# Another order of the feed-forward turns' steps, and two scratch tensors laid out in pieces of 1 KB

## What is computed

```python
x = x + attn(layernorm(x))        # _ska_block, itself with a residual
x = x + ffn(layernorm(x))         # 256 -> 1024 -> gelu -> 256, binarized weights

# attn, per chunk and head (Q, K, V: 128 x 64)
G = K.T @ K + 1e-4 * I
W = solve(G, K.T @ V)
U = I[:, :8]
for _ in range(2): U, _ = qr(W @ U)
Wr = U @ (U.T @ W)
S = 0.9 * S + Wr                   # state over the 8 chunks of a sequence
out = 0.125 * (Q @ S)
```

## Time and profile before

| | us |
|---|---|
| median of 3 runs | 900.69 |
| lowest and highest | 897.38, 904.1 |
| the profiled execution, its own time | 900.93 |
| its span | 899.1 |
| PE busy | 783.1 (87%) |
| DVE busy | 631.7 (70%) |
| ACT busy | 490.1 (55%) |
| POOL busy | 227.4 (25%) |

### The profile page before, as it was taken

One profiled execution on the slowest core, in us unless ns is written; L12 is line 12 of the kernel. 1 busy time (PEld: TensorE's weight loads), 2 busy tenths in 40 slices (PEclk: granted clock), 3 DMA queues, 4 the chain that ended last, 5 costly groups with the idle time before them and its releaser, 6 DMA issues.

```text
span 899.1 us, 34359 instructions
## 1 busy us (share of the span) xinstructions
PE 783.1 (87%) x14730; PEld 530.6 (59%) x14730; DVE 631.7 (70%) x1336; ACT 490.1 (55%) x1068; POOL 227.4 (25%) x297
## 2 busy tenths in 40 slices
PE   4999999999999998988687687888798888899996
PEld 2555555565555555656455565666576666677775
DVE  3666399089998999980798988889953304666664
ACT  1864444555455454554444465556566665466665
POOL 4666100201001100000201012652012203555554
PEclk9999999999999999999879888999999999899999
DMA  8555211653455636655734645344456432222210
GB/s 313 155 159 167 77 62 42 205 177 122 139 162 160 185 72 168 185 162 168 162 79 119 188 116 159 103 135 116 107 154 138 104 93 69 62 82 74 77 43 30
DMA packets 174662, 114.43 MB, mean 127 GB/s; under 512 B 134128, under 2 KB 152944, under 8 KB 173488
## 3 DMA queue, kind: packets, MB, share of 16 engines
q1 hardware_dynamic: 168784, 91.00, 36.8%
q0 software_dynamic: 5728, 21.24, 7.5%
HBM read 61.22 MB, written 50.99 MB: 125 GB/s over the span
## 4 chain that ended last, share of the span: by engine, by line
PE 66%; DVE 13%; issue 9%; DMA 5%; ACT 4%; SPq 1%; POOL 1%; POOLq 0%; DVEq 0%; ACTq 0%
PE psum L1286 25%; PE psum L1332 6%; PE psum L1531 6%; PE psum L1541 5%; DVE outer L1142 4%; PE psum L1473 3%; PE psum L1511 3%; DVE work L1148 3%; PE psum L1504 2%; PE psum L1388 2%; PE psum L1375 2%; PE psum L1362 2%; PE psum L1423 2%; DVE state L1204 2%; PE psum L1497 1%
## 5 line engine op out<-in xcount | busy, mean ns | idle before, releaser
L1286 PE MATMUL psum<-wkv,xhat 128*128 128x512 f32 x512 | 240.3, 613 | 4.3 <-ACT xhat L834 4.3
L1142 DVE SCALAR_TENSOR_TENSOR outer<-work,rd 128x992 f32<-128x992 f32 (+30 forms) x248 | 189.6, 764 | 8.9 <-DVE rd L1136 0.3
L1148 DVE TENSOR_TENSOR work<-work,outer 128x992 f32<-128x992 f32 (+30 forms) x248 | 176.3, 711 | 8.6
L1286 PEld LDWEIGHTS psum<-wkv,xhat 128*128 128x128 f32 x512 | 93.2, 192 | 105.3 <-issue 99.5
L871 ACT COPY kv<-psum 128x512 f32<-128x512 f32 x128 | 75.1, 587 | 120.8 <-PE psum L1286 120.5
L1002 ACT ACTIVATE late<-psum,b1c,alpha 128x128 f32<-128x128 f32 x256 | 96.7, 461 | 49.6 <-PE psum L1531 49.6
L759 POOL TENSOR_TENSOR hsplit<-late,hsplit 128x512 f16<-128x512 f32 x64 | 77.4, 1211 | 142.4 <-ACT hsplit L1007 142.3
L1531 PEld LDWEIGHTS psum<-y3t,s1t 128*128 128x128 f16 x1024 | 61.3, 102 | 17.7 <-issue 16.7
L1531 PE MATMUL psum<-y3t,s1t 128*128 128x128 f16 x1024 | 66.9, 227 | 4.4 <-DVE y3t L1232 4.0
L1541 PE MATMUL psum<-s2t,hsplit 128*128 128x256 f16 x512 | 63.7, 279 | 4.0 <-POOL hsplit L759 2.7
L1332 PE MATMUL psum<-kv 128*64 128x128 f32 x1024 | 64.4, 280 | 0.0
(11 more groups left out here) (130 smaller groups left out, 1279.5 us busy)
## 6 DMA issues: line engine op xcount, KB each, us to landing
gc_d<-gc SPq DMA_DIRECT2D x32, 384.0 KB, 2.5
schur_mem<-gc_d SPq DMA_DIRECT2D x32, 384.0 KB, 4.2
f_d<-late SPq DMA_DIRECT2D x16, 512.0 KB, 3.6
late<-f_d SPq DMA_DIRECT2D x32, 256.0 KB, 2.7
sv_d<-sv SPq DMA_DIRECT2D x16, 384.0 KB, 3.1
lead_d<-work POOLq DMA_DIRECT2D x4, 1024.0 KB, 5.0
schur_mem<-lead_d SPq DMA_DIRECT2D x32, 128.0 KB, 4.3
r_d<-pt SPq DMA_DIRECT2D x16, 256.0 KB, 2.2
```

What stands on the lines that cost most here:

```text
L1142: V.scalar_tensor_tensor(out=tile, in0=a[:, t, t + 1:HALF].unsqueeze(2).broadcast_to([P, m, HALF]), scalar=rd[:, t:t + 1], in1=a[:, t, t + ...
L1148: V.tensor_tensor(rest, rest, tile, ALU.subtract).then_inc(swept, 1)
L1286: ins = mm(dst[:], xnt[:, c, t], wkv[:, n, t, BANK * half:BANK * (half + 1)], start=t == 0, stop=t == KT - 1)
```

## The change

There are two parts.

**Order.** The turn's steps are appended in another sequence: AU (one chunk's operator) moves from behind GE0 to directly behind OUT; NB is taken one chunk further ahead (`r + 3`); X3 stands behind NB; and Y3 moves from behind AU to directly behind HID, ahead of GE0. Two DVE weights of the planner are larger. The mask step MB of a sequence waits in the plan until the NB steps of the sequence before last are placed. Since the planner interleaves all streams, the list changes from its 303rd PE step on.

**Layout.** `pt`, `r_d` and `rr` now hold the head index innermost, and `sv`, `sv_d` hold the 32-wide parts of a chunk first and the 64-wide parts behind, so that the reads of `rr` and `vv` are contiguous pieces of 1 KB per partition. For that SP and SX write PSUM with a step of 8 elements, SX and W read `pt` and `rr` with that step, `lt` is written by ACT with a step of 32 elements, and the copy of SV becomes two.

```diff
-DVE_WEIGHT = dict(AU=.75, AT=1.4, X3=.45, Y3=.5, OUT=.95)
+DVE_WEIGHT = dict(AU=.75, AT=1.4, X3=.8, Y3=.5, OUT=1.45)
-                if t <= now["pe"]:
+                if t <= now["pe"] and (b < 2 or ("NB", CPB * (b - 1) - 1) in where):
-        for step, n in (("LF", r + 4), ("LO1", r - 1), ("AT", r + 1), ("LR", r + 3), ("OUT", r - 2), ("X3", r + 1), ("NB", r + 2),
-                        ("HID", r), ("GE0", r), ("AU", r + 2), ("LO0", r), ("Y3", r + 1), ("GE1", r)):
+        for step, n in (("LF", r + 4), ("LO1", r - 1), ("AT", r + 1), ("LR", r + 3), ("OUT", r - 2), ("AU", r + 2), ("NB", r + 3),
+                        ("X3", r + 1), ("HID", r), ("Y3", r + 1), ("GE0", r), ("LO0", r), ("GE1", r)):
-    r_d = scratch("r_d", [NCH, P, PAIRS, HALF])
-    sv_d = scratch("sv_d", [NCH, P, PAIRS // 2, 3 * HALF])
+    r_d = scratch("r_d", [NCH, P, HALF, PAIRS])
+    sv_d = scratch("sv_d", [NCH, P, PAIRS // 2 * 3 * HALF])
...
-                    sp.dma_start(vv[:, i], sv_d[c + i][:, :, HALF:]).then_inc(solve_loaded, 16)
+                    sp.dma_start(vv[:, i], sv_d[c + i][:, P:].rearrange("p (s n) -> p s n", n=HD)).then_inc(solve_loaded, 16)
-                    sp.dma_start(rr[:, i, :, 0:HALF], r_d[c + i]).then_inc(sides_loaded, 16)
+                    sp.dma_start(rr[:, i, 0:HALF], r_d[c + i]).then_inc(sides_loaded, 16)
...
-                    nc.scalar.mul(lt[rows(2 * a)].rearrange("p c h n -> p (c h n)"), src[rows(2 * a)], -1.0)
+                    nc.scalar.mul(lt[rows(2 * a)].rearrange("p c h n -> p c n h"),
+                                  src[rows(2 * a)].rearrange("p (c n h) -> p c n h", c=2, h=PAIRS), -1.0)
-                nc.scalar.copy(sv[:].rearrange("p c s n -> p c (s n)"), pieces(place("SV", e), BANK)[:, :, 0:12 * HALF]
-                               ).then_inc(drain("SV", e), 1)
+                src = pieces(place("SV", e), BANK)[:, :, 0:12 * HALF].rearrange("p c (s n) -> p c s n", n=3 * HALF)
+                nc.scalar.copy(sv[:, :, 0:P].rearrange("p c (s n) -> p c s n", n=HALF), src[:, :, :, 0:HALF])
+                nc.scalar.copy(sv[:, :, P:].rearrange("p c (s n) -> p c s n", n=HD), src[:, :, :, HALF:]).then_inc(drain("SV", e), 1)
...
-                            ins = mm(dst[sl, at:at + HALF], lp[sl, c, h, HALF:], lp[sl, c, h, 0:HALF], start=True, stop=True)
+                            ins = mm(dst[sl, c, :, h], lp[sl, c, h, HALF:], lp[sl, c, h, 0:HALF], start=True, stop=True)
...
-                                r, u = rr[side(a), c % 2, 2 * q + n], cu[side(a), n, c % 2, q]
+                                r, u = rr[side(a), c % 2, :, 2 * q + n], cu[side(a), n, c % 2, q]
```

More of the change, by code:

```diff
@@ L374, in build @@
         w2n = schur_mem[:, FT * DM:FT * DM + KT * FF].rearrange("p (t h) -> p t h", h=FF)
-        pt = sb("pt", [P, 2, 2, PAIRS, HALF])
-        xg = pt[:].rearrange("p e c h n -> p (e c h n)").rearrange("p (a k d) -> p a k d", a=2, k=2)
+        pt = sb("pt", [P, 2, 2, HALF, PAIRS])
+        xg = pt[:].rearrange("p e c n h -> p (e c n h)").rearrange("p (a k d) -> p a k d", a=2, k=2)
         lt = sb("lt", [P, 2, PAIRS, HALF])
-        sv = sb("sv", [P, 2, PAIRS // 2, 3 * HALF])
+        sv = sb("sv", [P, 2, PAIRS // 2 * 3 * HALF])
         lps = sb("lps", [P, 2, PAIRS // 2, HD])
         vv = sb("vv", [P, 2, PAIRS // 2, HD])
-        rr = sb("rr", [P, 2, PAIRS, HD])
+        rr = sb("rr", [P, 2, HD, PAIRS])
         cu = sb("cu", [P, 2, 2, PAIRS // 2, HD])
@@ L562, in load_solve @@
                 if e == 0:
-                    sp.wait_ge(eyes_placed, 4)
+                    sp.wait_ge(eyes_placed, 6)
                 if e % HALF_BATCH == 0:
@@ L618, in _ @@
                     sp.wait_ge(*is_drained("SX", c))
-                    sp.dma_start(r_d[2 * c:2 * c + 2].rearrange("c p h n -> p c h n"), pt[:, c % 2]
+                    sp.dma_start(r_d[2 * c:2 * c + 2].rearrange("c p n h -> p c n h"), pt[:, c % 2]
                                  ).then_inc(r_stored[c % 2], 16)
@@ L622, in _ @@
                     sp.wait_ge(*is_drained("SV", c))
-                    sp.dma_start(sv_d[2 * c:2 * c + 2].rearrange("c p s n -> p c s n"), sv[:]).then_inc(sv_stored, 16)
+                    sp.dma_start(sv_d[2 * c:2 * c + 2].rearrange("c p n -> p c n"), sv[:]).then_inc(sv_stored, 16)
                 elif step == "LS":
@@ L709, in load_sweep @@
                     for s in range(PAIRS // 2):
-                        src = sv_d[CPB * b:CPB * (b + 1), :, s, 0:HALF].rearrange("c (q i) n -> (c q) i n", q=QUADS)
+                        src = sv_d[CPB * b:CPB * (b + 1), :, HALF * s:HALF * (s + 1)].rearrange("c (q i) n -> (c q) i n", q=QUADS)
                         pool.dma_start(buf[rows(s), :, 0:HALF], src).then_inc(sweep_loaded[j], 16)
@@ L800, in place_eyes @@
                     eye = ident[sl, sl].unsqueeze(1).broadcast_to([HALF, 2 * PAIRS, HALF])
-                    nc.scalar.copy(rr[sl, :, :, HALF:].rearrange("p a h n -> p (a h) n"), eye).then_inc(eyes_placed, 1)
+                    for i in range(2):
+                        nc.scalar.copy(rr[sl, i, HALF:], ident[sl, sl].unsqueeze(2).broadcast_to([HALF, HALF, PAIRS])
+                                       ).then_inc(eyes_placed, 1)
                     nc.scalar.copy(lt[sl].rearrange("p a h n -> p (a h) n"), eye).then_inc(eyes_placed, 1)
@@ L894, in leading_inverse @@
                 wait(act, r_stored[e % 2], 16 * (e // 2))
-                nc.scalar.copy(pt[:, e % 2].rearrange("p c h n -> p (c h n)"), place("SP", e)).then_inc(drain("SP", e), 1)
+                nc.scalar.copy(pt[:, e % 2].rearrange("p c n h -> p (c n h)"), place("SP", e)).then_inc(drain("SP", e), 1)
             def crosses(e):
@@ L902, in crosses @@
                 for a in range(2):
-                    nc.scalar.mul(lt[rows(2 * a)].rearrange("p c h n -> p (c h n)"), src[rows(2 * a)], -1.0)
+                    nc.scalar.mul(lt[rows(2 * a)].rearrange("p c h n -> p c n h"),
+                                  src[rows(2 * a)].rearrange("p (c n h) -> p c n h", c=2, h=PAIRS), -1.0)
                 for a in range(2):
-                    ins = nc.scalar.mul(pt[rows(2 * a + 1), e % 2].rearrange("p c h n -> p (c h n)"), src[rows(2 * a + 1)], -1.0)
+                    ins = nc.scalar.mul(pt[rows(2 * a + 1), e % 2].rearrange("p c n h -> p (c n h)"), src[rows(2 * a + 1)], -1.0)
                 ins.then_inc(drain("SX", e), 1)
@@ L1354, in leading_inverse @@
             def leading_inverse(e):
-                dst = begin("SP", e)
+                dst = begin("SP", e).rearrange("p (c n h) -> p c n h", c=2, h=PAIRS)
                 pe.wait_ge(schur_loaded[e % 2], 64 * (e // 2 + 1))
@@ L1369, in crosses @@
                     for h in range(PAIRS):
-                        at = HALF * (PAIRS * c + h)
                         for turned in range(2):
@@ L1373, in crosses @@
                                 sl = rows(2 * a)
-                                p, b = pt[sl, e % 2, c, h], gct[sl, e % 2, c, h, 0:HALF]
-                                ins = mm(dst[rows(2 * a + turned), at:at + HALF], b if turned else p, p if turned else b,
+                                p, b = pt[sl, e % 2, c, :, h], gct[sl, e % 2, c, h, 0:HALF]
+                                ins = mm(dst[rows(2 * a + turned), c, :, h], b if turned else p, p if turned else b,
                                          start=True, stop=True)
@@ L1380, in complements @@
                 if e == 0:
-                    pe.wait_ge(eyes_placed, 4)
+                    pe.wait_ge(eyes_placed, 6)
                 dst = begin("SV", e)
```

3 lines of the change are left out of this document (1 added, 2 removed).

## The result

The changed kernel takes **935.70 us** (median of 4 runs, 934.31 to 941.37) against 899.04 (4 runs, 893.63 to 904.10): a ratio of 1.042, 95% interval 1.034 to 1.050, so it is slower. The prediction said 935 with a range of 898 to 970. The sum came out right, but not every term of it: two errors of about 15 us, of opposite sign, cancel. Their medians are of all runs of a kernel and their ratios of its fast runs alone, so the two can differ by most of a percent.

A forecast was written before the change was run, and what follows sets the result against it. PE bound most of the kernel (66% of the chain), with latency the risk in the turns; 646 + 237.4 + 32.2 - 8 + 23 + 2 = 932.7 us of span, so 935 us, range 898 to 970.

The forecast's parts named there:

- Decay wait, and what comes late next: In the turns, PE's 0.65 us wait before AT goes; what is late next must be followed round the turn's loop.
- The loop of Y3: From Y3 to Y3 through ACT, GpSimd and DVE: 8.0 us per turn instead of 7.09, +23 us, +2 at the end.
- the ring: High half, both GELU halves with casts, LO1, power, X3, Y3, high half: a closed chain of 7.98 us per turn.
- PE's own work per turn: In the stretch of turns alone, PE works 6.44 us of each 7.09 us turn.
- Where the eighth sweep ends: DVE's last sweep, freed of turn work, ends at 646 us, 15.7 earlier; ends of the range 634 and 661.7.
- What PE still has to do then: After the eighth sweep: 237.4 us as before, five more turns 32.2, fewer solve steps -8.
- Layout: Shorter `rr` loads, extra ACT copies and steps of 8 elements in matmuls: 0 in all; matmul upper end 83 us.
- Strided matmuls cost: Rival: PSUM rows written in steps of 8 go at half rate, SP and SX add 48 us: 983 us; chance 0.12.
- The ring does not close: Rival: power reaches X3 in time, turns are gapless on PE, 34 us of idle go: 901 us; chance 0.17.
- The sweeps gain more: Rival: small inverse's input there at once, eighth sweep ends near 620, loop of Y3 still binds: 909 us; chance 0.09.

The follow-up runs named there:

- `order_only`: The kernel before with the new sequence, weights and mask rule, in the old layout: 918.33 us, ratio 1.019.
- the ring was cut: LO1 of chunk r - 1 moved behind AT of chunk r + 1: 904.52 us on the kernel after, 887.93 us with the new order in the old layout.
- `sv` alone: The kernel before with only `sv` and `sv_d` in the new layout, no matmul with a step: 899.32 us, ratio 0.989.

## Why the prediction came out as it did

**Decay wait, and what comes late next: right.** The wait on the state's decay is gone from PE's waits and one on X3 stands in its place, 1.42 us per turn.

**The loop of Y3: right.** 7.77 us against the 8.0 of the sum. Every link was within 0.02 us of its row but one: power to X3 took 0.58 instead of 0.76. That one move of one step takes the turn to 6.16 is what shows the ring; that it was order and not layout, `order_only` shows.

**PE's own work per turn: 5% too high.** I took 7.09 - 0.65 = 6.44; a turn without a gap takes 6.16. The starts show where the 0.28 us are: in the row of before, Y3's 0.38 us count in full because a gap follows, while AT starts 0.22 us behind Y3 where none does (0.16 us); OUT starts 0.87 us behind AT instead of 0.94, and what follows OUT 1.75 us behind it instead of 1.84, with AU 0.05 longer. It did not matter, since the ring lay above both.

**Where the eighth sweep ends: 6 us off, and right by accident.** The forecast was 646, the trace has 652.41; alone, the order gives 635.95. The step that failed is that the seventh sweep starts where it did, at 495.88. With the layout it starts at 502.27, and at 503.09 and 507.39 in the two other kernels that have it; with the old layout it starts between 486.30 and 499.82 in eleven traces (488.17 with the order alone). The sixth sweep already tells old from new layout: it starts between 423.97 and 434.60 in the eleven traces where SX reads without a step, mean 429.1, and at 437.00, 439.88 and 442.47 in three of the new one, mean 439.8. From the seventh sweep's end to the eighth's start I had 25.7 us (553.3 to 579) where it was 29.3 (559.15 to 588.49): the fetch of the small inverse waited 8.64 us behind the sweep's end, and the store of SV came late on SP's queue: the prediction followed GpSimd's list to the sweep's loads and not SP's, where that store stands behind LR. The sweep itself took 63.9 us against 66.7.

**What PE still has to do then: right.** 237.4 + 32.2 - 8 + 23 + 2 = 286.6 us against 282.3. With 7.77 for 8.0 in 22 rings the sum gives 281.5.

**Layout: the wrong term, put at 0.** I took 0 with an upper end of 83 us; it is 17 to 19 us (917.74 against 898.89 alone, 935.70 against 918.33 on top of the order). The sentence that failed is "half the columns save nothing, so columns do not set the time of SP, and a slower stream may hide there". It holds for SP, whose step is in the *written* PSUM and which did take 1.13; I carried it over to SX and W, whose step is in the operands read from SBUF. Those took 2.2 and 1.9 where the prediction named 1.9 and 1.1 as what would be seen. The 1.9 for SX was a misreading besides: 84 is how many records the chain showed, and the step with all its 128 matmuls took about 1.3 us before. Of some 40 us of longer steps (32 W by 0.8, 16 SX by 0.9), 28 show as busy time of PE, and 17 to 19 reach the end. ACT was put at 0 as well, for the second copy of SV alone; the step of 32 elements in which `lt` is written was left out, and it costs 32 x 0.48 = 15 us of ACT, of which PE waits for some 7 to 9.

**The rivals.** "Strided matmuls cost" was the one that spoke of this term, and it blamed PSUM: there it is refuted, since SP writes at its old rate. By the Trainium skill (PSUM — Partial Sum Buffer, Specifications (TRN2)) a non-contiguous pattern would have slowed SP too; the measured 195 ns against 192 decides against that for a step of 8 fp32 elements (with the order alone, and no step, it is 195 too). "The ring does not close" would have been seen as a Y3 every 6.5 us, which only came when the ring was cut. "The sweeps gain more" did not come: it wanted the eighth sweep's end near 620, and the order alone gives 635.95, between that and the forecast.

So the total is made of turns 3 us too long (286.6 against the 283.2 of the order alone), sweeps 10 us too late (646 against 635.95, give or take the 5 us between traces), and a layout some 17 us too cheap. The range would have held the time without the luck; the point would not have been hit.

**Open.** How the 17 to 19 us split between SX, the copy `lt` and W was not separated. PE's longer waits behind `lt` suggest 7 to 9 us for that copy, but no kernel had it alone. One trace speaks against a cost of W up to the eighth sweep: with both its operands in steps of 4 it has all of W's cost, and yet its sixth sweep starts at 429.52 and its eighth ends at 658.9, no later than in the kernel before. Whether `sv` alone gains anything is open too.

## What to carry over

When a step is moved on one engine, walk the loop of the whole turn through every engine's list, not only the one that idles: if both halves of a stage end up between a value and its own successor, that ring can exceed the engine's work, and one move on a third engine (here LO1 behind AT on GpSimd) can open it. Separate where a step is written from where it is read before carrying a row over: a strided write into PSUM told nothing of a strided read by a matmul. And a total that comes out right proves no term: run the halves alone.

## What the runs showed of the hardware

A matmul of 64 by 64 fp32 pays 30 to 60 ns when an operand is read from SBUF in steps of 16 or 32 bytes (stationary from 230 to 286 ns, or to 262 and 264 where the moving one has a step too; moving from 224 to 285), its weight load 64 (140 to 204); steps of 8 bytes are free (229 and 223), as is a PSUM write in steps of 32 bytes (SP, 195 against 192). ACT's 32x512 fp32 copy goes from 588 to 1064 ns when it writes in steps of 128 bytes. A read of 128 KB in pieces of 1 KB instead of 128 bytes lands in 2.4 us instead of 3.8 (medians; 2.4 to 2.5 and 3.3 to 3.8 over the traces).
